# Index loads of the edge attention interleaved with destination rows on SyncE

## What is computed

```python
# layer 0 (4 heads; edge list = (src, dst))
h = (x @ W).reshape(N, HEADS, HEAD_DIM)
e = leaky_relu(a_src[src] + a_dst[dst], 0.2)
m = segment_max(e, dst); e = exp(e - m[dst])
alpha = e / segment_sum(e, dst)[dst]
out = segment_sum(alpha[:, :, None] * h[src], dst)

# layer 1 (1 head, an edge term in the score)
x_t = x @ W2.T
f = concatenate([x[src], edge_attr], -1) @ W1.T
score = leaky_relu((x * att_r).sum(-1)[dst] + (f * att_l).sum(-1))
alpha = softmax of score over the edges of each dst
h = segment_sum(x_t[src] * alpha[:, None], dst)
```

## Time and profile before

| | before |
|---|---|
| median of 3 runs | 5386.51 us |
| the profiled execution | 5389.08 us |
| its span, first to last instruction | 5387.1 us |
| TensorE matmul busy, share of the span | 4039.5 us, 75% |
| VectorE busy | 2565.4 us, 48% |
| GpSimd busy | 2179.4 us, 40% |
| ScalarE busy | 1551.4 us, 29% |
| granted TensorE clock, mean | 0.74 |
| gathers (L684) | 1856, 1928.9 us busy |

### The profile page before, as it was taken

The page is one execution under the profiler, slowest core; times in us unless marked ns, Lnnn a source line. Parts: engine busy times, 40 slices in busy tenths (PEclk is TensorE's granted clock), DMA queues, the critical chain, the costliest instruction groups (busy, mean ns, idle before and its releaser), DMA issues. The chain is left out here.

```text
span 5387.1 us, 88957 instructions
## 1 busy us (share of the span) xinstructions
PE 4039.5 (75%) x21808; PEld 3103.1 (58%) x21809; DVE 2565.4 (48%) x8219; ACT 1551.4 (29%) x4325; POOL 2179.4 (40%) x2095
## 2 busy tenths in 40 slices
PE   5177777777777768866377776667766899999999
PEld 3155555555555557744255444445544688888888
DVE  7266666666666775545244344444444542122121
ACT  2122222222222213322122222222222333333333
POOL 0366666666666013246555555555555000000000
PEclk9566666666666559977566666666666899999999
DMA  3233333333335214434333333333335100000000
GB/s 100 69 83 80 82 81 81 81 82 81 80 81 76 80 48 161 159 97 111 76 79 76 77 77 76 77 79 75 76 76 76 53 6 6 6 6 6 5 5 8
DMA packets 382428, 367.94 MB, mean 68 GB/s; under 512 B 249324, under 2 KB 309388, under 8 KB 382242
## 3 DMA queue, kind: packets, MB, share of 16 engines
q0 software_dynamic: 107072, 272.84, 20.3%
q1 hardware_dynamic: 272774, 92.39, 7.1%
q10 hardware_dynamic: 2396, 0.84, 0.1%
HBM read 324.13 MB, written 41.59 MB: 68 GB/s over the span
## 5 line engine op out<-in xcount | busy, mean ns | idle before, releaser
L684 POOL DMA_INDIRECT g_G<-rows,g_pack x1856 | 1928.9, 1039 | 1453.4 <-PE bank L717 725.4
L717 PE MATMUL bank<-g_G,g_MB 128*125 128x260 f32 x1856 | 769.6, 585 | 58.3 <-DVE g_G L939 28.8
L769 PE MATMUL bank<-g_rhs,g_MT 125*128 125x16 bf16 (+1 forms) x5568 | 217.1, 169 | 786.6 <-issue 577.2
L924 DVE SCALAR_TENSOR_TENSOR acc<-acc,g_c,bank 125x65 f32 (+1 forms) x2320 | 622.7, 317 | 332.6 <-PE bank L717 283.5
L717 PE MATMUL bank<-g_G,g_M 128*125 128x257 f32 x1856 | 741.1, 568 | 8.7 <-issue 3.6
L790 ACT ACTIVATE g_mt_d<-bank,unode 125x256 bf16<-125x256 f32 x928 | 384.1, 464 | 1044.9 <-PE bank L702 542.8
L717 PEld LDWEIGHTS bank<-g_G,g_MB 128*125 128x125 f32 x1856 | 520.2, 294 | 272.7 <-issue 143.4
L769 PEld LDWEIGHTS bank<-g_rhs,g_MT 125*128 125x128 bf16 x5568 | 181.7, 101 | 852.0 <-issue 625.6
L717 PEld LDWEIGHTS bank<-g_G,g_M 128*125 128x125 f32 x1856 | 506.6, 287 | 197.0 <-issue 42.0
L1366 DVE SCALAR_TENSOR_TENSOR X<-bank,e_cw,X 125x256 f32 (+1 forms) x400 | 175.2, 479 | 845.0 <-PE bank L1192 845.0
L1262 ACT ACTIVATE e_h<-bank,e_bi_c,e_sc_c 128x250 f32<-128x250 f32 x800 | 403.6, 555 | 559.6 <-PE bank L1183 421.6
(11 more groups left out here) (300 smaller groups left out, 4400.2 us busy)
## 6 DMA issues: line engine op xcount, KB each, us to landing
g_G<-rows,g_pack POOLq DMA_INDIRECT x1856
acc<-in_edge_attr SPq DMA_DIRECT2D x50, 531.2 KB
g_pack<-edge_pack SPq DMA_DIRECT2D x928, 2.0 KB
g_drow<-edge_dst SPq DMA_DIRECT2D x928, 1.0 KB
expert_out<-x_y SPq DMA_DIRECT2D x54, 256.0 KB
g_qe<-edge_q SPq DMA_DIRECT2D x464, 1.0 KB
rows<-acc SPq DMA_DIRECT2D x25, 253.9 KB
rows<-n_T SPq DMA_DIRECT2D x25, 251.0 KB
```

The source lines that it names most:

```text
L684: nc.gpsimd.indirect_dma_start(G[:, r, q, :], None, rows_d[l], bass.IndirectOffsetOnAxis(ap=pack[:, r, q, 0:1], axis=0)).then_inc(S(p + f" ...
L717: mm_ = nc.tensor.matmul(sum_bank(u)[0:TN, 0:HW], left, G[:, rk, q, :], start=(c == 0), stop=(c == C - 1))
L769: mm_ = nc.tensor.matmul(Xe_ps[:, q * KM * H:(q + 1) * KM * H], MT[:, turn(r, 1, q // CP), q % CP, :], rhs[:, q // C, s, :, :], start=(s = ...
L924: ins = nc.vector.scalar_tensor_tensor(at, at, c1[:, rk, u, h:h + 1], sum_bank(u)[0:TN, h * W:(h + 1) * W], ALU.mult, ALU.add)
```

## The change

In SyncE's slot the two loops over the 8 units become one. For each unit the load of the destination row of group i-1 is issued first, and right behind it the loads of `pack` (and in layer 1 `qe`) of group i. The wait for `spread` stays ahead of each pair of destination rows, so it now also stands ahead of the pair's index loads. Both register loads come ahead of the loop. Transfers, sizes, waits and semaphores are the same, and the other engines' code is unchanged.

```diff
                         if has(i, 0):
                             sp.reg_load(regs[0], unit_i[0:1, bass.ds(i * U, U)])
-                            for u in range(U):
+                        if has(i, 1):
+                            sp.reg_load(regs[1], unit_i[0:1, bass.ds(i * U - U, U)])
+                        for u in range(U):
+                            if has(i, 1):
+                                s = sp.snap(regs[1][u], min_val=0, max_val=E)
+                                v_ = u // 2
+                                if u % 2 == 0 and late(i, 2):
+                                    after(sp, p + "spread", i * V - 2 * V + (v_ + 1))
+                                    held(sp, p + "spread_seen")
+                                sp.dma_start(drow[:, u, :], dst_d[:, bass.ds(s, UE)]).then_inc(S(p + f"drow_in{(r - 1) % RING}"), 16)
+                            if has(i, 0):
                                 s = sp.snap(regs[0][u], min_val=0, max_val=E)
                                 sp.dma_start(pack[:, r, u * C:(u + 1) * C, :],
                                              pack_d[bass.ds(s, UE), :].rearrange("(p c) k -> p c k", p=P)).then_inc(S(p + f"pack_in{r}"), 16)
                                 if l == 1:
                                     sp.dma_start(qe[:, r, u * C:(u + 1) * C],
                                                  q_d[bass.ds(s, UE)].rearrange("(p c) -> p c", p=P)).then_inc(S(p + f"q_in{r}"), 16)
-                        if has(i, 1):
-                            sp.reg_load(regs[1], unit_i[0:1, bass.ds(i * U - U, U)])
-                            for u in range(U):
-                                s = sp.snap(regs[1][u], min_val=0, max_val=E)
-                                v_ = u // 2
-                                if u % 2 == 0 and late(i, 2):
-                                    after(sp, p + "spread", i * V - 2 * V + (v_ + 1))
-                                    held(sp, p + "spread_seen")
-                                sp.dma_start(drow[:, u, :], dst_d[:, bass.ds(s, UE)]).then_inc(S(p + f"drow_in{(r - 1) % RING}"), 16)
                     run(sp, slot)
```

## The result

The changed kernel takes 5957.32 us (median of four runs, 5947.58 to 5963.03) against 5386.96 for the kernel before (four runs) beside it: a ratio of 1.105, 95% interval 1.103 to 1.108, or 570 us more. The prediction was 5534, in a range of 5230 to 5790.

What follows compares the result with a forecast made beforehand. Each attention stage was taken as a chain of 58 slots, TensorE slowed beside unbroken gathers. 5389.1 + 108 (layer 1) + 40 (layer 0) = 5537, less 2.6: 5534 us, range 5230 to 5790.

Steps and rivals of the forecast that it cites:

- Xe's gap: Layer 1, a slot's last 48 matmuls: steps of 1.42 us beside gathers; their going gains up to 6.3 us.
- third part: Gathers become one run of 16 over the next slot's head, slowing TensorE; 108 us lost in layer 1, 40 in layer 0.
- the sign of being wrong: Layer 1's V block (L753) keeping 2.3 us and starting 9.5 us in: third part wrong, slot shorter than now.
- the step that failed: Layer 0: between a gain of 0.8 and a loss of 6.5 us a slot, a loss of 0.7 taken, 40 us.
- layer 0 starves too: Rival, chance 0.15: layer 0's first half starves as in layer 1, 6.5 us a slot, 370 us; 5865 to 5900.
- a term too small: Layer 1's slot goes from 27.9 to 29.8 us, with SyncE's floor at 29.1: 1.9 by 57 = 108 us.
- The landing: Layer 1, from a load's issue to the gather it releases: 1.2 us, between bounds of 0.3 and 1.4.
- second part: VectorE's `dloc`, 20.5 us into layer 1's slot, barely waits: cost 0, up to 2 us a slot if SyncE slows.
- first part: GpSimd's first gather, 20.2 us into layer 1's slot, 11 later; rows there at 44, wanted at about 55: costs nothing.
- The gap in Xe simply goes: Rival, chance 0.25: layer 1's Xe loses its gap, the slot's first half isn't starved; 5120 to 5260 us.
- nothing: Rival, chance 0.10: loads had 11 us to spare, the first half gives back what Xe gains; 5380 to 5400 us.

Runs made afterwards that it cites:

- starved set: Set of runs made together in which the kernel before, unedited, had a median of 5382 to 5420 us.
- free sets: Sets of runs made together in which the kernel before, unedited, had a median of 4809 to 4821 us.
- ahead: Changed kernel, but the interleaved index loads are those of the group after, one slot ahead: 4805.33 us, ratio 0.9995; starved, in layer 0 alone, 27.56 us a slot.
- pair_waits: Changed kernel with a semaphore for each pair's index loads, GpSimd waiting pair by pair: 4803.24 us, ratio 0.999, free; 5361.76 us starved.

## Why the prediction was wrong

*The direction.* The change does put 16 gathers into one run over the head of the next slot, Xe's gap goes by it, and the head loses more than that. The first gather of a group stands 32 us after the start of the slot in which its loads go out (the forecast had 20, and 25 to 30 by its third part), because the starving holds back SyncE as well.

*The third part's mechanism was wrong.* I had TensorE itself run short: some 40 matmuls at hand, then one per 1.42 us, and so the fourth spread of layer 1 between 17 and 22.4 us into the slot. I had also named the sign of being wrong: a V block that keeps its 2.3 us and starts 9.5 us in, with a slot shorter than before. The block did just that (over 53 slots of the trace it starts at 9.3 us and lasts 2.1, medians), and the fourth spread ends at 14.0 us against 12.0 before. Yet the slot grew by 3.57 us. What costs is not late work of TensorE but that VectorE, ScalarE and SyncE go on late after it: 13 us after the V block in the slot shown. That the direction of layer 1 came true is in that part luck.

*Layer 0: the step that failed.* I had both bounds (a gain of 0.8, a loss of 6.5 us a slot) and took a loss of 0.7, since 46 of 48 matmuls passed inside a run there. Measured: 6.55. The nearest row was the wrong one. It was mild because VectorE's work stretched the gathers; at the slot's head VectorE waits for TensorE, so nothing stretches them (1398.31 is the last of eleven starts 1.25 to 1.30 us apart). What eases the starving is itself starved. The rival "layer 0 starves too", at 0.15, had this term right at 370 us (373 measured). That its bound met the measurement to 0.1 us is partly luck: it came from a fourth spread at 21 us in place of 14.6, and the trace has it at 22.6 in place of 14.4 (means), with TensorE waiting for VectorE and not for its own instructions.

*Layer 1: a term too small.* 1.9 us forecast, 3.57 measured. Two sizes were off. The end of the starving I took as 2.65 us behind the last gather's start, from TensorE's own matmuls; VectorE and SyncE go on 3.9 and 4.1 us behind it. And I let 16 of SyncE's 24 loads go out during the run at 1.32 us each; 12 did, six of them up to 4.2 us apart, so 12 were left in place of 8. The 1.32 us were the mild rows: beside the gathers of the very slot of the earlier trace rows SyncE stepped by 2.1 us in the kernel before too:

```profile
3019.89 0.01 SPq L655 DMA_DIRECT2D g_pack<-edge_pack  x1
3022.03 0.70 SPq L658 DMA_DIRECT2D g_qe<-edge_q  x1
3024.15 0.00 SPq L655 DMA_DIRECT2D g_pack<-edge_pack  x1
```

The landing was misread, without harm. The gather at 3032.39 was not released by the load at 3030.96: its idle time is the 0.30 us of every gather in a row, and that load is `qe`, for which GpSimd doesn't wait. Where a gather does wait (3371.03), it starts 2.45 us behind the last `pack` load and 1.9 behind the `qe` load after it; the sum had 1.7 for the latter (0.5 of issue and 1.2).

*First and second part: cost nothing.* In the starved set both hold: `b` of the changed kernel waits 20.4 us for rows in the whole trace, and `dloc` 0.4 and 0.9 us in the slots shown. In the free sets the slot is 21 us, and the first part's sum is what binds: 46 against 42. I had written its condition, "if the rate of everything else stays", and not what it costs where the slot is short.

*The rivals.* "The gap in Xe simply goes" and "nothing" fell. For the first I had set the Trainium skill, page "Runtime: NRT & Kernel Launch", section "Instruction fetch mechanics", by which fetching ahead stays hidden, and held the steps of 1.42 us against it. They don't speak against it: from 2900 to 4100 us of the kernel before, where 337.6 us of Xe's idle time are "issue", the profile records no packet on the queues that it names "instruction", and none from 3250 to 4650 us of the changed kernel, where VectorE waits 599.4 us at L1027 for "remote". So no fetch that the profile records is the cause there. The other rule I had weighed, the Trainium skill, page "DMA: Bandwidth & Descriptors", section "Rules for kernel authors", to issue early and wait late, agrees with the runs: in the free set `ahead`, which issues the loads a slot earlier, and `pair_waits` each give back all that late indices cost; in a starved set `pair_waits` does, and `ahead` was run in layer 0 alone, where it does nearly.

*What the forecast rested on without saying so.* Every row came from one trace, and 576 us of its two attention stages, almost a fifth, were the starving. In a free set the change ends at 4874.

*Open.* What makes a set starved. Where a set has several runs, all are of its kind, the kernel before as the changed one. The granted clock differs little (0.64 and 0.63 in the earlier trace rows, 0.67 and 0.69 free), and TensorE's busy time by 125 of the 580 us; 44 to 48 GB/s of extra traffic of the kernel's own don't make it. What else ran on the same chip or machine isn't on record and was not tested. Whether instructions or semaphores travel late, the traces can't tell.

## What to carry to other kernels

Idle time that the profile calls "issue" or "remote", with nothing waited for, should be looked up in a second trace, from another set of runs, before a forecast rests on it. A consumer that waits for all parts of a batch should wait for each part by itself as soon as the producer's order is stretched. And when a term has two far bounds, ask whether what made the nearest row mild will still be there after the change.

## What the runs showed of the hardware

The same program takes 5382 to 5420 us in some sets of runs and 4809 to 4821 in others, with TensorE's busy time the same within 4% (4039.5 and 3914.5 us). In the former, beside 16 gathers at 1.25 us each, VectorE went on 13 us after the block of TensorE that it waited for was over, and SyncE's issues stepped by up to 4.2 us; the profile records no fetch of instructions there. A pause of 1.4 us behind each fourth gather took 2.3 us off layer 1's slot (27.98 to 25.69). In the latter, with 91% of the gathers' starts in layer 1 at most 1.5 us apart, none of Xe's idle time is "issue".
